# A linear-attention stage unrolled in turns of 16 slots

## The chip, the cores and the metric

The kernel runs on one core of one Trainium2 chip. The metric is the device time of one execution in microseconds (us), lower is better. A core has five engines with a queue each: TensorE (PE, matmuls; its weight loads are shown as PEld), VectorE (DVE), ScalarE (ACT), GpSimd (POOL) and SyncE (SP), which here only issues DMA transfers. Engines run side by side and wait for each other through semaphores. Each takes its own instructions strictly in the order of its list, so an instruction that waits holds up all behind it.

## What is computed

A decoder layer on x of shape (2, 2048, 512) in float32: linear attention, cross attention to a context of 154 keys, and a mixture of experts, each on a layer norm of its input and added to it. The change touches the first of the three:

```python
qkv = x @ w_qkv                                   # x is layer-normed
q, k, v = split(qkv), 16 heads of 32
q_proj = elu1(einsum('bhnd,hdf->bhnf', q, proj))  # elu1(x) = x + 1 if x > 0 else exp(x); 128 features
k_proj = elu1(einsum('bhnd,hdf->bhnf', k, proj))
kv     = einsum('bhnf,bhnd->bhfd', k_proj, v)
attn   = einsum('bhnf,bhfd->bhnd', q_proj, kv)
z      = 1 / (einsum('bhnf,bhf->bhn', q_proj, k_proj.sum(2)) + 1e-8)
out    = (attn * z) @ w_out + b_out
x      = x + out
```

## The kernel before

Four stages follow each other, each in a block of its own with its own semaphores: `project`, `attend_linear`, `attend_cross`, `experts`. `project` writes the queries of all tokens to DRAM and leaves kv and the key sums in SBUF. The 4096 tokens are 8 blocks of 512 (`NBLK`), four of each batch element.

`attend_linear` (L614) handles one block as follows.
- **Head** (L969): one matmul of the features' weights with the queries of a head (16 per block) into a PSUM bank. ACT takes relu(-x) (L771) and its exponential (L776) into a tile `e`; DVE adds max(x, 0) (L841) into `qp`.
- **Group** (L989, L983): for four heads, numerators and denominators, 8 matmul instructions each.
- **Divide** (L844): DVE adds 1e-8, takes the reciprocal (L848) and splits it into a high and a low part. Products in reduced precision are made from such parts: high x high, high x low, low x high (`PASSES`), so one product of four chunks is 12 matmuls.
- **Spread** (L1002): PE spreads the reciprocals over the rows, 8 matmuls; DVE multiplies the numerators by them (L860), ACT makes the high part (L787) and DVE the low part (L864) of `u_att`.
- **Output** (L1006): four tiles of 12 matmuls with `wo`; DVE adds each to x (L871) and takes its mean and variance (L873 to L878), POOL the power -1/2 (L761), DVE normalises (L884).
- **Transposes** (L1019): PE transposes each normalised tile, ACT and DVE make its high and low part (L791, L890).
- **Queries** of the cross attention (L1055): four groups of 12 matmuls with `wq`; DVE adds the bias (L921), SP stores all of them at once.

The order is written out by hand. A prologue does block 0 up to the spreading. Each `turn(i)` (L1023 on PE, L893 on DVE, L794 on ACT) then does output, transposes and queries of block i, and between them, in pairs, the heads of block i + 1, its groups, division and spreading. Turns run in loops of three (`Fori`) and one written out. All PSUM jobs but numerators and denominators go round four banks; PE waits until DVE has read the job four before. SP loads the queries of a block, 3 x 1 MB, when the heads of the block before are all computed (L739), and x of a block when its rows are normalised (L737). Semaphores are raised by one at the start of the stage in a block of their own (`prime`), since loops wait on register values.

Of the kernel before, what the change touches and what calls it, by code (L numbers as in the profile page):

```python
# [18 lines left out]
F32 = mybir.dt.float32  # L19
F32R = mybir.dt.float32r  # L20
# [129 lines left out]
def decoder_kernel(nc, a, out):  # L150
# [11 lines left out]
    with ExitStack() as whole:  # L162
# [4 lines left out]
        with ExitStack() as linear:  # L167

            kv_w = linear.enter_context(nc.sbuf_tensor("kv_w", [P, NB, H, HD], F32))
            ks_w = linear.enter_context(nc.sbuf_tensor("ks_w", [P, NB, H, HD], F32))  # L170
            project(nc, a, NBLK, BLK, x_blk, q_dram, ident, kv_w, ks_w, half, stage)
            attend_linear(nc, a, NBLK, BLK, x_blk, q_dram, x1_dram, xq_dram, ident, kv_w, ks_w, half, stage)
# [5 lines left out]
def project(nc, a, NBLK, BLK, x_blk, q_dram, ident, kv_w, ks_w, half, stage):  # L178
# [59 lines left out]
    with ExitStack() as ctx:  # L238
# [7 lines left out]
        f_w = sb("f_w", [3 * HD, H, F], F32R)  # L246
# [38 lines left out]
        with nc.Block() as block:  # L285
            @block.sync
            def _(sp):
# [32 lines left out]
                for i in range(-1, NBLK - 1):  # L320
# [4 lines left out]
                    if i == 0:  # L325
                        sp.wait_ge(w_lo, 3)
                        sp.dma_start(stage[0:3 * HD, 0:H * F], a["features3"]).then_inc(next_in, 16)
# [7 lines left out]
                sp.wait_ge(next_in, 48)  # L335
# [278 lines left out]
def attend_linear(nc, a, NBLK, BLK, x_blk, q_dram, x1_dram, xq_dram, ident, kv_w, ks_w, half, stage):  # L614

    qp_pair = lambda n: [("QP", 2 * n), ("QP", 2 * n + 1)]
    JOBS = (qp_pair(0) + [("O", 0)] + qp_pair(1) + [("O", 1)] + qp_pair(2)
            + [("O", 2)] + qp_pair(3) + [("T", 0), ("O", 3)] + qp_pair(4) + [("T", 1)] + qp_pair(5) + [("T", 2)]
            + qp_pair(6) + [("T", 3)] + qp_pair(7) + [("XQ", 0), ("XQ", 1), ("XQ", 2)]
            + [("R", g) for g in range(G)] + [("XQ", 3)])
    POS = {key: n for n, key in enumerate(JOBS)}
    LAST_POS = {key: n for n, key in enumerate(j for j in JOBS if j[0] not in ("QP", "R"))}
    NJ, BANKS, QSLOTS, ESLOTS = len(JOBS), 4, 8, 4  # L630
    FIRST = H + G
    assert NJ % BANKS == 0 and FIRST % BANKS == 0
    with ExitStack() as ctx:
# [3 lines left out]
        def sem(name):  # L637
            return primed(ctx, nc, sems, "li_" + name)

        sems = []  # L640
        f_w = sb("f_w", [3 * HD, H, F], F32R)
        wo = sb("wo", [P, 2, C, D], F32R)
        wq = sb("wq", [P, 2, C, D], F32R)
        spread_raw = sb("spread_raw", [P, G, P])
# [10 lines left out]
        e = sb("e", [P, ESLOTS, TB])  # L655
        num = sb("num", [P, G, TB])
        den = sb("den", [P, 2, TB])
        xq = sb("xq", [P, G, TB])
# [3 lines left out]
        pause = sb("pause", [P, 1])  # L662
        bank = [ctx.enter_context(nc.psum_tensor(f"li_bank{n}", [P, 512], F32)) for n in range(BANKS)]
        p_num = [ctx.enter_context(nc.psum_tensor(f"li_p_num{n}", [P, 512], F32)) for n in range(2)]
        p_den = ctx.enter_context(nc.psum_tensor("li_p_den", [P, 512], F32))

        w_hi, w_lo, const_in, next_in = sem("w_hi"), sem("w_lo"), sem("const_in"), sem("next_in")
        x_in, q_in, x1_out, xq_out = sem("x_in"), sem("q_in"), sem("x1_out"), sem("xq_out")
        q0_in = [sem(f"q0_in{g}") for g in range(G)]
        filled, dve_read = sem("filled"), sem("dve_read")  # L670
        relu_set, exp_set, heads_used = sem("relu_set"), sem("exp_set"), sem("heads_used")
        num_full, num_taken, den_set, rec_set = sem("num_full"), sem("num_taken"), sem("den_set"), sem("rec_set")
        norm_hi, norm_lo, turn_hi = sem("norm_hi"), sem("norm_lo"), sem("turn_hi")
        xb_set, stats_set, aggr_set, var_set = sem("xb_set"), sem("stats_set"), sem("aggr_set"), sem("var_set")
        rstd_set, xn_set = sem("rstd_set"), sem("xn_set")
        prime(nc, pause, sems)

        f_raw = stage[0:3 * HD, 0:H * F].rearrange("p (h f) -> p h f", h=H)

        def pos(turn):  # L680
            return LAST_POS if isinstance(turn, int) and turn == NBLK - 1 else POS

        def job(turn, key):

            return FIRST + NJ * turn + pos(turn)[key]

        def bank_of(turn, key):
            return bank[pos(turn)[key] % BANKS]

        def is_first(block):  # L690
            return isinstance(block, int) and block == 0

        def ahead(block, key):

            return key[1] + H * (key[0] == "R") if is_first(block) else job(block - 1, key)

        def bank_ahead(block, key):
            return bank[key[1] % BANKS] if is_first(block) else bank_of(block - 1, key)

        def turns(engine, body):  # L700

            for b in range(NBLK // BLK):
                with engine.Fori(0, BLK - 1) as k:
                    body(k + BLK * b, b, True)
                body(BLK * b + BLK - 1, b + 1, b + 1 < NBLK // BLK)

        with nc.Block() as block:
            @block.sync
            def _(sp):
                def load_q(i):  # L710
                    for r, part in enumerate((HI, LO, HI)):
                        sp.dma_start(q3[r * HD:(r + 1) * HD].bitcast(F32).rearrange("p h t -> p (h t)"),
                                     q_dram[i, part]).then_inc(q_in, 16)

                for g in range(G):
                    for r, part in enumerate((HI, LO, HI)):
                        cols = slice(g * HG * TB, (g + 1) * HG * TB)
# [26 lines left out]
                with sp.Fori(0, NBLK - 2) as i:  # L744
                    turn(i, 2)
# [1209 lines left out]
```

## Time and profile before

| | us |
|---|---|
| Median of 3 runs | 2795.8 (2794.68 to 2798.59) |
| Profiled execution | 2796.93 |
| Its span, first to last instruction | 2795.2 |
| PE busy over the span | 2638.4 (94%) |
| DVE, ACT, POOL busy | 1361.0, 858.0, 299.1 |
| Mean granted clock of PE | 0.959 |

The span is that of the profiled execution; the profile's times below are us from its start. The page shows PE busy nearly throughout, but the share is a mean over four stages. The slices of the linear stage, from about 460 to 845 us, have PE at 7 to 9 tenths, the ones of `experts` behind 1250 us at 9. A busy PE is also not always a fast one: the granted clock is 1.00 (2.4 GHz) or 0.50 (1.2 GHz), and a mean in between says that the stretch held both.

### The profile page before, as it was taken

What the parts mean: (1) busy time and instruction counts of PE and PEld (TensorE: products, weight loads), DVE (VectorE), ACT (ScalarE), POOL (GpSimd) and SP (SyncE); (2) the same over time, 40 slices, a digit from 0 to 9 for tenths busy, and PEclk for the clock granted to TensorE, in tenths of its full rate; (3) what the DMA queues carried; (4) which work ended last, traced back from release to release, by engine and by line L of the source; (5) the groups of instructions that cost most, each with busy time, mean ns of one, the idle gap of its engine ahead of it and who ended that gap; (6) DMA issues with size and microseconds to landing.
All of it is one profiled execution on the core that took longest, in us unless ns stands there. A gap on an engine that the chain in (4) does not pass through costs nothing. (4 is left out here: it accounts for less than half of the span.)

```text
span 2795.2 us, 34765 instructions
## 1 busy us (share of the span) xinstructions
PE 2638.4 (94%) x12656; PEld 1945.0 (70%) x12680; DVE 1361.0 (49%) x2100; ACT 858.0 (31%) x1364; POOL 299.1 (11%) x228
## 2 busy tenths in 40 slices
PE   7999997899896999799969999999998999999999
PEld 6777774556564554555458888888886888888887
DVE  4544434777765554655463344343335434334433
ACT  3555456455532332133221221111112121112111
POOL 1444343111110111111100000000000000000000
PEclk9999995999997999799989999999999999999999
DMA  6646434554613111212140000000113100000001
GB/s 193 170 98 148 107 87 113 158 156 115 166 75 110 61 54 45 92 61 91 46 155 23 23 23 32 36 23 23 45 45 136 42 26 23 23 23 23 23 23 60
DMA packets 61396, 207.62 MB, mean 74 GB/s; under 512 B 8592, under 2 KB 10384, under 8 KB 50192
## 3 DMA queue, kind: packets, MB, share of 16 engines
q1 hardware_dynamic: 61008, 205.59, 24.4%
q8 instruction: 63, 1.03, 0.2%
q0 software_dynamic: 288, 0.69, 0.1%
q14 instruction: 37, 0.30, 0.0%
HBM read 123.05 MB, written 58.72 MB: 65 GB/s over the span
## 5 line engine op out<-in xcount | busy, mean ns | idle before, releaser
L1876 PE MATMUL ex_pg<-ex_x,ex_w 128*128 128x512 f32 x3840 | 885.5, 390 | 3.3 <-DVE ex_lt L1759 3.3
L1876 PEld LDWEIGHTS ex_pg<-ex_x,ex_w 128*128 128x128 f32 x3840 | 723.3, 188 | 153.7 <-issue 3.5
L1891 PE MATMUL ex_pd<-ex_w,ex_ht 128*128 128x512 f32 x1920 | 446.6, 389 | 0.0
L1825 DVE TENSOR_TENSOR ex_h<-ex_s_g,ex_pg 128x512 f32<-128x512 f32 x160 | 110.1, 688 | 648.6 <-PE ex_pg L1876 647.7
L1891 PEld LDWEIGHTS ex_pd<-ex_w,ex_ht 128*128 128x128 f32 x1920 | 360.5, 188 | 74.7
L1732 ACT ACTIVATE ex_s_g<-ex_pg 128x512 f32<-128x512 f32 x160 | 95.8, 599 | 748.7 <-PE ex_pg L1876 748.6
L1797 DVE SCALAR_TENSOR_TENSOR ex_acc<-ex_pd,ex_share,ex_acc 128x512 f32<-128x512 f32 x320 | 234.4, 748 | 90.3 <-PE ex_pd L1891 84.9
L546 PE MATMUL pr_pj<-pr_xt,pr_w 128*128 128x512 f32 x768 | 194.5, 402 | 4.3 <-DVE pr_xt L443 4.2
L359 POOL TENSOR_TENSOR pr_ks_sum<-pr_ks_sum,pr_kp 128x512 f32<-128x512 f32 x128 | 164.5, 1286 | 228.2 <-DVE pr_kp L490 226.4
L490 DVE SCALAR_TENSOR_TENSOR pr_kp<-pr_pk,pr_kp 128x512 f32<-128x512 f32 x128 | 88.6, 692 | 179.5 <-ACT pr_kp L407 179.1
L546 PEld LDWEIGHTS pr_pj<-pr_xt,pr_w 128*128 128x128 f32 x768 | 142.1, 192 | 33.5 <-issue 2.2
L1263 ACT ACTIVATE cr_ring<-cr_s_bank 128x512 f32<-128x512 f32 x160 | 95.8, 599 | 202.7 <-remote 104.0
L1735 ACT CAST ex_ht<-ex_h 128x512 fp32r<-128x512 f32 x160 | 98.6, 616 | 181.4 <-DVE ex_h L1825 181.4
L1482 PE MATMUL cr_s_bank<-cr_xq,cr_k_w 128*128 128x512 f32 x480 | 151.7, 429 | 0.0
L1329 DVE TENSOR_REDUCE cr_mx<-cr_bank 128x4 f32<-128x512 f32 (+1 forms) x160 | 105.7, 688 | 93.9 <-PE cr_bank L1456 65.8
L404 ACT ACTIVATE pr_kp<-pr_pk 128x512 f32<-128x512 f32 x128 | 76.7, 599 | 133.9 <-PE pr_pk L576 126.8
L1828 DVE TENSOR_TENSOR ex_ht<-ex_h,ex_ht 128x512 fp32r<-128x512 f32 x160 | 110.4, 690 | 6.7
L1534 PE MATMUL cr_bank<-cr_wo,cr_u 128*128 128x512 f32 x384 | 99.9, 406 | 5.7 <-DVE cr_u L1398 5.7
L957 PE MATMUL li_bank<-li_u_ln,li_wq 128*128 128x512 f32 x384 | 97.4, 407 | 8.4 <-DVE li_u_ln L890 8.4
L1482 PEld LDWEIGHTS cr_s_bank<-cr_xq,cr_k_w 128*128 128x128 f32 x480 | 88.6, 193 | 22.0 <-issue 7.7
L841 DVE SCALAR_TENSOR_TENSOR li_qp<-li_bank,li_e 128x512 f32<-128x512 f32 x128 | 82.8, 685 | 33.7 <-ACT li_e L776 29.0
L543 PE MATMUL pr_pj<-pr_w,pr_xt 128*128 128x512 f32 x384 | 99.2, 400 | 0.0
(175 smaller groups left out, 2856.1 us busy)
## 6 DMA issues: line engine op xcount, KB each, us to landing
stage<-in_units SPq DMA_DIRECT2D x21, 1536.0 KB, 6.6
pr_k<-pr_kq SPq DMA_DIRECT2D x192, 128.0 KB, 2.5
li_q<-q_scratch SPq DMA_DIRECT2D x21, 1024.0 KB, 12.2
q_scratch<-pr_kq SPq DMA_DIRECT2D x128, 128.0 KB, 2.4
x_scratch<-cr_x SPq DMA_DIRECT2D x16, 1024.0 KB, 4.8
pr_x<-in_x SPq DMA_DIRECT2D x8, 1024.0 KB, 6.4
li_x<-in_x SPq DMA_DIRECT2D x8, 1024.0 KB, 5.2
x_scratch<-li_x SPq DMA_DIRECT2D x8, 1024.0 KB, 3.9
```

What stands on the lines that cost most here:

```text
L359: nc.gpsimd.tensor_tensor(part, part, slot(step), ALU.add).then_inc(ks_step, 1)
L543: mm = nc.tensor.matmul(out[:], xt[:, s, c, cols], w[:, m, 2, c], start=(n == 0), stop=(n == MM - 1))
L546: mm = nc.tensor.matmul(out[:], w[:, s, "QK".index(kind), c, cols], xt[:, m, c], start=(n == 0), stop=(n == MM - 1))
L1329: nc.vector.tensor_reduce(dst, src, AX.X, ALU.max).then_inc(dve_read, 1)
L1482: nc.tensor.matmul(s_bank[n % SBANKS][:], k_w[:, s, g, j * P:(j + 1) * P], q[:, m, g], start=(c == 0), stop=False)
L1534: mm = nc.tensor.matmul(bank_of(k, "O", t)[:], u[:, s, g, t * P:(t + 1) * P], wo[:, m, g], start=(n == 0), stop=(n == 3 * G - 1))
L1735: nc.scalar.copy(ht[:, s % 2, HI, f], h[:, f]).then_inc(ht_hi, 1)
L1797: nc.vector.scalar_tensor_tensor(acc[:, n], pd[t][:], share[:, n, bass.ds(e + s // BLK, 1)], acc[:, n], ALU.mult, ALU.add).then_inc(d_take ...
L1825: nc.vector.tensor_tensor(h[:, f], s_g[:, f], pg[2 * f + 1][:], ALU.mult).then_inc(h_set, 1)
L1828: nc.vector.tensor_tensor(ht[:, s % 2, LO, f], h[:, f], ht[:, s % 2, HI, f].bitcast(F32), ALU.subtract).then_inc(ht_lo, 1)
L1876: mm = nc.tensor.matmul(pg[2 * f + which][:], w[:, slot, sp_, col:col + P], x3[:, m, k, c * TB:(c + 1) * TB], start=(n == 0), stop=(n == 3 ...
L1891: mm = nc.tensor.matmul(pd[t][:], ht[:, s % 2, sp_, f, t * P:(t + 1) * P], w[:, slot, m, WD + f * D:WD + (f + 1) * D], start=(n == 0), sto ...
```

## The change

`attend_linear` is rewritten. There is no prologue and no loop: `turns` walks i from -1 to 8, and each turn has 16 slots. Slot s of turn i holds head s of block i + 1, and besides it parts of the output work of block i and of the queries of block i - 1. PE's part of each slot is in `PLAN`; the numbers are (kind, index, first matmul, last matmul):

```diff
+    PLAN = {
+        0: [("XQ", 0, 0, 8)],
+        1: [("ND", 3), ("XQ", 0, 8, 11)],
+        2: [("XQ", 0, 11, 12), ("XQ", 1, 0, 7)],
+        3: [("XQ", 1, 7, 12), ("XQ", 2, 0, 3)],
+        4: [("XQ", 2, 3, 12)],
+        5: [("R", 0), ("R", 1), ("R", 2)],
+        6: [("ND", 0), ("R", 3), ("XQ", 3, 0, 6)],
+        7: [("XQ", 3, 6, 12)],
+        8: [("O", 0, 0, 9)],
+        9: [("O", 0, 9, 12), ("O", 1, 0, 6)],
+        10: [("ND", 1), ("O", 1, 6, 9)],
+        11: [("O", 1, 9, 12), ("O", 2, 0, 6)],
+        12: [("O", 2, 6, 12), ("O", 3, 0, 3), ("T", 0)],
+        13: [("O", 3, 3, 12), ("T", 1)],
+        14: [("ND", 2), ("T", 2)],
+        15: [("T", 3)],
+    }
```

XQ are queries of block i - 1, ND is a group (of block i + 1, but group 3 of block i), R spreading, O output tiles and T transposes of block i. On PE a slot begins with its head:

```diff
+                def slot(i, s, ahead, now, behind):
+                    if ahead:
+                        head(i + 1, s)
+                    for job in PLAN[s]:
...
```

DVE's slot has the head first and then the rest of the slot:

```diff
+                def slot(i, s, ahead, now, behind):
+                    if s == 0 and behind:
+                        turned(i - 1, TT - 1)
+                    if ahead:
+                        n = H * (i + 1) + s
+                        dve.wait_ge(exp_set, n + 1)
+                        nc.vector.scalar_tensor_tensor(qp[:, n % QSLOTS], h_bank[n % HBANKS][:], 0.0, qp[:, n % QSLOTS],
+                                                       ALU.max, ALU.add).then_inc(qp_set, 1)
...
+                    if now:
+                        if s in (2, 3):
...
+                            reciprocal(i, s - 2)
+                        if s == 3:
+                            reciprocal_low(i, 0)
+                        if s == 4:
+                            reciprocal_low(i, 1)
+                        if s in (5, 6, 7):
+                            for g in ((0, 1), (2,), (3,))[s - 5]:
+                                normalise(i, g)
+                        if s in (10, 12, 13, 14):
+                            add_out(i, (10, 12, 13, 14).index(s))
+                        if s in (11, 13, 14, 15):
+                            norm(i, (11, 13, 14, 15).index(s))
+                        if s in (13, 14, 15):
+                            turned(i, s - 13)
```

ACT does relu and exponential of a head one right after the other, into `qp` itself (the tile `e` is gone), and takes over the high part of the reciprocal and the queries' bias:

```diff
+                        nc.scalar.activation(qp[:, n % QSLOTS], h_bank[n % HBANKS][:], ACT.Relu, scale=-1.0)\
+                            .then_inc(relu_set, 1)
+                        act.wait_ge(relu_set, n + 1)
+                        nc.scalar.activation(qp[:, n % QSLOTS], qp[:, n % QSLOTS], ACT.Exp, scale=-1.0)\
+                            .then_inc(exp_set, 1)
+                    if i == -1 and s == 6:
+                        nc.scalar.copy(wo[:, HI], staged(stage, 1)).then_inc(wo_hi, 1)
+                    if i == 0 and s == 0:
+                        nc.scalar.copy(wq[:, HI], staged(stage, 2)).then_inc(wq_hi, 1)
...
+                    if now and s == 2:
+                        take_num(i, G - 1)
+                    if behind and s in (3, 4):
+                        query(i - 1, s - 3)
+                    if now and s in (3, 4):
+                        reciprocal_high(i, s - 3)
+                    if behind and s == 5:
+                        query(i - 1, 2)
+                    if now and s in (5, 6, 7):
+                        for g in ((0,), (1, 2), (3,))[s - 5]:
+                            normalised(i, g)
+                    if behind and s == 8:
+                        query(i - 1, 3)
+                    if ahead and s in (8, 11, 15):
+                        take_num(i + 1, (8, 11, 15).index(s))
+                    if now and s in (13, 14, 15):
+                        turned(i, s - 13)
```

POOL takes the low part of `u_att` from DVE. The rest:
- Heads have two PSUM banks of their own (`HBANKS`), all other jobs share three (`BANKS`) instead of four for both.
- The reciprocal is taken in two halves of 256 columns, slots 2 and 3.
- SP loads the queries of block i + 2 in four parts, in slots 4, 8, 12 and 15 of turn i, each when the heads that used that part are computed; it stores the queries of the cross attention in four parts, in slots 3, 4, 5 and 8; x goes out in slot 14 and the next x comes in in slot 15.
- `f_w`, the features' weights split in two parts, is kept from `project` instead of being loaded and split again, and the priming block of this stage is gone.

```diff
+                    if behind and s in (3, 4, 5, 8):
+                        query_out(i - 1, (3, 4, 5, 8).index(s))
+                    if i >= 0 and i + 2 < NBLK and s in (4, 8, 12, 15):
+                        load_q(i + 2, (4, 8, 12, 15).index(s))
```

## Rows read from the trace of the kernel before

**Rows 1.** Busy times of one turn: length, PE, PEld, DVE, ACT, POOL, clock, DMA.

```profile
545.70:590.50 44.80, 41.08 (x200) 25.62 (x201) 34.19 (x61) 23.40 (x44) 7.53 (x5) 0.96 0.53 140
```

**Rows 2.** PE's waits from 480 to 845 us: total, times, longest.

```profile
PE li_bank L969 <- DMA li_q<-q_scratch: 8.9, 7, 1.7
PE li_bank L957 <- DVE li_u_ln L890: 8.4, 8, 1.4
```

**Rows 3.** Timeline of PE, one turn: start, length, instruction, idle before.

```profile
545.75 0.72 PE L969 MATMUL li_bank<-li_q,li_f_w 96*128 96x512 f32 x2 [1.52 <-DMA li_q<-q_scratch]
...
562.11 1.06 PE L989 MATMUL li_p_num<-li_qp,kv_w 128*32 128x512 f32 x8
562.99 1.04 PE L983 MATMUL li_p_den<-li_qp,ks_w 128*32 128x512 f32 x8
563.96 0.66 PE L1019 MATMUL li_bank<-ident,li_xn 128*128 128x128 f32 x4
564.37 1.10 PE L969 MATMUL li_bank<-li_q,li_f_w 96*128 96x512 f32 x2
...
584.30 2.00 PE L1002 MATMUL li_bank<-li_rec,li_spread 128*128 128x512 f32 x8
586.14 2.95 PE L957 MATMUL li_bank<-li_u_ln,li_wq 128*128 128x512 f32 x12
590.51 0.73 PE L969 MATMUL li_bank<-li_q,li_f_w 96*128 96x512 f32 x2 [1.42 <-DMA li_q<-q_scratch]
```

**Rows 4.** The same view, the last turn.

```profile
810.74 8.57 PE L957 MATMUL li_bank<-li_wo,li_u_att 128*128 128x512 f32 x36
819.14 0.60 PE L1019 MATMUL li_bank<-ident,li_xn 128*128 128x128 f32 x4
...
826.13 0.63 PE L1019 MATMUL li_bank<-ident,li_xn 128*128 128x128 f32 x4 [0.42 <-DVE li_xn L884]
828.16 14.21 PE L957 MATMUL li_bank<-li_u_ln,li_wq 128*128 128x512 f32 x48 [1.40 <-DVE li_u_ln L890]
```

**Rows 5.** Timeline of ACT and of DVE in the project stage.

```profile
301.99 0.60 ACT L404 ACTIVATE pr_kp<-pr_pk 128x512 f32<-128x512 f32 x1 [1.35 <-PE pr_pk L576]
302.63 0.63 ACT L407 ACTIVATE pr_kp<-pr_kp 128x512 f32<-128x512 f32 x1
...
303.29 0.69 DVE L490 SCALAR_TENSOR_TENSOR pr_kp<-pr_pk,pr_kp 128x512 f32<-128x512 f32 x1 [0.97 <-ACT pr_kp L407]
```

**Rows 6.** Timelines of PE and ACT: a head and its relu, twice.

```profile
549.11 0.63 PE L969 MATMUL li_bank<-li_q,li_f_w 96*128 96x512 f32 x2
...
549.54 1.09 ACT L771 ACTIVATE li_e<-li_bank 128x512 f32<-128x512 f32 x2 [1.14 <-PE li_bank L969]
...
463.59 2.04 PE L969 MATMUL li_bank<-li_q,li_f_w 96*128 96x512 f32 x4 [9.07 <-DMA li_q<-q_scratch]
...
464.39 1.09 ACT L771 ACTIVATE li_e<-li_bank 128x512 f32<-128x512 f32 x2 [4.68 <-PE li_bank L969]
```

**Rows 7.** Timeline of DVE: an output tile added, its normalisation, and one later.

```profile
557.90 0.69 DVE L871 TENSOR_TENSOR li_x<-li_x,li_bank 128x512 f32<-128x512 f32 x1 [1.80 <-PE li_bank L957]
...
559.71 0.54 DVE L884 TENSOR_SCALAR li_xn<-li_x,li_mv,li_rstd 128x512 f32<-128x512 f32 x1
...
825.45 0.54 DVE L884 TENSOR_SCALAR li_xn<-li_x,li_mv,li_rstd 128x512 f32<-128x512 f32 x1
```

**Rows 8.** Groups of instructions: count, busy, mean ns of one, idle before.

```profile
L359 POOL TENSOR_TENSOR pr_ks_sum<-pr_ks_sum,pr_kp 128x512 f32<-128x512 f32 x128 | 164.5, 1286 | 228.2 <-DVE pr_kp L490 226.4
...
L758 POOL TENSOR_TENSOR li_x<-li_x,li_bias 128x2048 f32<-128x2048 f32 x8 | 36.7, 4592 | 84.9 <-DMA li_x<-in_x 84.9
L848 DVE RECIPROCAL li_den<-li_den 128x512 f32<-128x512 f32 x8 | 26.8, 3353 | 0.3
```

**Rows 9.** As rows 1, two stretches of 3 us of the last turn.

```profile
825.70:828.70 3.00, 1.18 (x6) 0.92 (x6) 1.67 (x3) 1.17 (x2) 0.00 (x0) 0.79 0.29 120
828.70:831.70 3.00, 3.00 (x8) 2.31 (x7) 0.00 (x0) 0.00 (x0) 0.00 (x0) 0.50 0.00 0
```

## Prediction: what the slots make of the time

> **What bounds the kernel now.** I read the busy time by turn first, then the waits of TensorE (PE), then the timelines of PE, ScalarE (ACT) and VectorE (DVE) over one turn. Only the linear-attention stage changes, so only that stage is costed. Its first head product starts at 463.59 us [rows 6] and its last turn starts at 810.74 us [rows 4]. A full turn takes 590.51 - 545.75 = 44.8 us [rows 3], with PE busy 41.1 of it and DVE only 34.2 [rows 1]: PE is the bound, with gaps. The gaps that recur are the wait for the queries' load (8.9 us in seven turns) and the wait for the low part of the normalised rows (8.4 us in eight) [rows 2]. The six turns from 545.75 to 810.74 mean 44.2 us.
>
> PE's own work in a turn, by start to start: the output product and the queries are 96 matmuls at (819.14 - 810.74)/36 = 0.233 us [rows 4], so 22.5. Sixteen heads at the same pace are 3.8. A group of four heads costs 0.88 for numerators and 0.97 for denominators [rows 3], four groups 7.4. Four transposed tiles at 0.41 [rows 3] are 1.7. Spreading the reciprocals takes 1.84 [rows 3]. Sum 37.2 us; so about 7 us of each turn is gap or half clock, which is all that this change could win per turn.
>
> **The change part by part.** The PE work is the same 37.2 us, reordered. What decides is what each slot waits for.
>
> *Loads.* Queries now come in four parts, each requested as soon as its heads are consumed. The load wait (about 1.3 us a turn [rows 2]) goes to nothing, hidden behind three quarters of a turn. Query outputs go out in quarters, from ACT instead of DVE: four operations of 0.6 us more, and ACT was busy 23.4 of 44.8 us [rows 1]. SyncE's list mixes these stores, which wait for ACT, with the loads; the store of x stands last in the turn and behind it the next input, which is wanted some 20 us later, so nothing in that queue is late.
>
> *The new head step.* Per head, ACT does relu, then the exponential on the same tile at once, then DVE adds. The project stage does exactly this: relu to exponential 0.64 us, exponential to DVE 0.66 us [rows 5]. A head product starts 0.43 us before its relu at full clock and 0.80 at half clock [rows 6]. So DVE can take head s 1.73 us after PE started it and is free about 0.60 later: at +2.33. In DVE's list of a slot the head comes first, and everything else of the slot queues behind it.
>
> *Slots 13 and 14.* Adding an output tile, with its statistics, takes 559.71 - 557.90 = 1.81 us and the normalisation 0.54 more [rows 7]. In slot 13 DVE does head, output tile 2, normalisation of tile 1; PE in the same slot wants the transpose of tile 1. It may start at 2.33 + 1.81 + 0.54 + 0.14 = 4.8 us (0.14 for the semaphore, estimated from 825.99 to 826.13 in the last turn, where the normalisation ends and the transpose starts [rows 4, 7]). PE has only 0.23 + 9 x 0.233 = 2.3 us to do until then: stall 2.5. Slot 14 has the same pattern (output tile 3, normalisation 2, transpose 2) against a head and a group, 2.1 us: stall 2.7.
>
> *Slot 15 and the hand-over.* Head, normalisation 3, transpose 3: 2.33 + 0.54 + 0.14 = 3.0 us against a head alone, 0.23: stall 2.8. From the start of the last transpose to the queries that need its low part takes 828.16 - 826.13 = 2.0 us [rows 4], minus 0.6 of transpose and head: stall 1.4, what the kernel before pays too.
>
> *Slot 12.* Transpose 0 needs the bank of output tile 1, which DVE frees at slot start + 2.33 + 0.7 = 3.0; PE arrives at 2.3: stall 0.7.
>
> *Slots 2 to 5.* DVE's chain is head 2 (ready 1.73 after its start), denominator 0.7, half a reciprocal 1.7 (3.353 for a whole one [rows 8]), head 0.6, the other half 1.7, a low part 0.4, head 0.6, low part 0.4: the spreading product may start 8.5 us after slot 2 began. PE has slots 2 to 4 (6.6 us) and one head, so 6.8: stall 1.7. Slot 9 waits for the last low part of the attention result, now on GpSimd (POOL): four of 1.29 us, by the row of the same shape [rows 8]. The last starts after head 7, its multiplication on DVE and its cast on ACT, about 5.0 us after slot 7 began at 18.6: done by 23.6 us of the turn, against 22.8 at which PE asks. Stall 0.8.
>
> Sum of a turn at full clock: 37.2 + 0.7 + 2.5 + 2.7 + 2.8 + 1.4 + 1.7 + 0.8 = 49.8 us.
>
> *The clock.* In the last turn of before PE was busy 1.18 of 3 us, and the next 3 us were granted 0.50 (1.2 GHz of 2.4) [rows 9]; the 48 query matmuls at that place took 14.2 us against 11.2 at the pace above [rows 4]. Slots 13 to 15 now hold 6 us of work in 15.5, so I take the fall in every turn: 3.0 for the queries and 2 x 0.37 for later relus. A turn then takes 53.5; I take 53, since a fall that comes late costs less. The Trainium skill (TensorE: Matmul & The Clock Gate, section on oscillation) says that gaps between bursts of matmuls drop the clock and each new burst pays for the ramp. By that rule this order, meant to be denser or not, loses; the row of the last turn agrees.
>
> *Start.* The weights of the head product are no longer split again, but PE waited for the queries' load at that time [rows 6], so nothing; one block of semaphore priming goes, my estimate 1.5 us (bounds 0 and 3, as the gap between two stages is all that holds it). Only two head banks remain: head product to free bank is 0.80 + 0.64 + 0.66 + 0.73 = 2.83 us at half clock, so 1.42 a head, and each group (3.6 at half clock, by twice the rows of a group [rows 3]) stops the heads for about 2: 16 x 1.42 + about 4 = 27 us to turn 0. In turn 0 the split of the queries' weights on DVE (2.4 us, an estimate from 0.69 for a quarter of the columns [rows 5]) and the reciprocal chain come before the spreading: about 15 us, then 13 to slot 9, then 28 for slots 9 to 15 as above. The first query product starts 84 us after the first head. Before has its block 0 and turn 0 done, queries included, 545.75 - 463.59 = 82.2 us after it.
>
> *End.* Turn 7 has no heads: queries of block 6 (14.2), a group 1.85, spreading 1.84, 0.4 waiting, then outputs and transposes as in the last turn, 828.16 - 810.74 = 17.4: 35.7. The last queries take 14.2, as before. The last output is a quarter and lands about 1.5 us earlier.
>
> **The total.** -1.5 + 84 + 6 x 53 + 35.7 + 14.2 - 1.5 = 449 us. Before, the same stretch is 842.4 - 463.6 = 379 (the last queries start at 828.16 and take 14.21 [rows 4]). The difference is +70 us. The profiled execution took 2796.9 us (span 2795.2); the median is 1.1 below, so 2796.9 + 70 - 1.1 = 2866 us.
>
> **Rivals.**
> *The clock holds.* The same stalls without half clock: a turn of 49.8, turn 7 at 32.7, the start 2 us shorter: +70 - 19 - 3 - 2 = +46, so 2842 us. Against: rows 9. Chance 0.12.
> *The chain is tighter than I think* (faster than before). The mechanism: head products are answered ahead of PE, so that DVE reaches slots 13 to 15 early and PE finds its transposes ready. It decides from a turn of 41.3 us, where -1.5 + 84 + 6T + 35.7 + 14.2 - 1.5 equals 379; that leaves at most 4 us a turn for stalls and half clock. If the gaps of slots 13 to 15 and the clock loss vanish and the rest stays, a turn is 37.2 + 0.7 + 1.4 = 39.3, and turn 0 is some 8 us shorter: -20, so 2776 us. For it: PE was 92% busy in a turn already [rows 1], and loads are ahead. Against: PE issues head s in slot s and DVE cannot pass it; the slots' order is fixed on all engines. Chance 0.05, and 0.03 that it stops half-way, within 0.2%.
> *POOL collides.* The input's bias addition (4.6 us [rows 8]) and the low parts share POOL, and it also runs beside DVE. I reckon that it ends about 6 us before the first low part of the attention result is wanted. If the next input lands 10 us later, that margin is gone and slot 9 waits 4 us more in six turns: +24, 2890 us. The Trainium skill (SBUF — State Buffer, on the port pair shared by VectorE and GpSimd) says a DVE operation with two inputs in SBUF and a GpSimd operation that reads it exclude each other. By that rule the two short low parts of the reciprocal could wait for the addition, up to 4.6 us a turn, and the time would be 2866 + 6 x 4.6 = 2894 us as an estimate from that page. No row here has the two together. Chance 0.08.
> The forecast itself: 0.72.
>
> **How the numbers follow.** The range of 8 in 10 takes the forecast's own bounds (a turn from 51 to 56, so -12 and +18, start from 80 to 88) and the case of the held clock: 2836 to 2890. The chances: slower 0.92, same 0.03, faster 0.05. A difference under 0.2% is about what a measurement here cannot tell from none.
>
> **What would show it.** In the changed profile: turns (from one first query product to the next) of about 53 us; PE waiting for DVE's normalised tile (the transposes) for about 8 us a turn, by far its largest wait, three times a turn; the spreading product waiting 1.7 us for the reciprocal's low part; no wait for the queries' load; a granted clock of half at the end of each turn. A turn below 45 us, or transposes that do not wait, would prove the walk through the slots wrong.

## The result and the profile after

The changed kernel takes 2876.75 us (median of 6 runs, 2873.7 to 2881.31) against 2797.65 (2794.68 to 2799.49) on the same chip: ratio 1.0285, interval 1.0272 to 1.0298. It is slower by 79 us; the forecast was 70, and 2876.75 lies inside the range. Its profiled execution has a span of 2876.6 us (before 2795.2). By stages:

| us, profiled execution | before | after | difference |
|---|---|---|---|
| first head product | 463.59 | 463.61 | 0.0 |
| from there to the first product of cross attention | 396.1 | 482.9 | +86.8 |
| cross attention, to the first product of `experts` | 568.6 | 560.1 | -8.5 |
| `experts` | 1367.0 | 1370.0 | +3.0 |

PE's waits in the linear stage (total, times, longest), which answer to [rows 2]:

```profile
PE li_bank L998 <- DVE li_xn L889: 47.6, 23, 2.7
PE li_h_bank L952 <- DVE li_qp L904: 22.5, 11, 8.2
PE li_bank L976 <- DVE li_rec L862: 11.0, 7, 2.1
PE li_bank L1011 <- DVE li_u_ln L895: 9.3, 8, 1.5
PE li_bank L989 <- POOL li_u_att L771: 6.9, 8, 1.9
PE li_h_bank L952 <- DMA li_q<-q_scratch: 6.6, 1, 6.6
PE li_bank L998 <- DVE li_x L875: 4.5, 7, 0.7
```

In the changed kernel L998 is the transposes, L952 a head, L976 the spreading, L1011 the queries, L989 the output. No turn waits for the queries' load any more; the 6.6 us are the wait ahead of the stage's first head, 9.1 us in the kernel before [rows 6]. The transposes now wait 23 times for the normalised tile, 47.6 us in all. The busy times of one turn, as in [rows 1]:

```profile
555.69:610.11 54.42, 43.81 (x201) 27.46 (x201) 28.92 (x53) 28.52 (x51) 12.45 (x9) 0.88 0.57 176
```

The turn takes 54.4 us instead of 44.8. PE's busy time grew by 2.7 us though its work is the same, and the clock is 0.88 instead of 0.96. The end of that turn on PE, slots 12 to 15 (start, length, instruction, idle before it and who ended it), against [rows 3]:

```profile
592.69 0.66 PE L998 MATMUL li_bank<-ident,li_xn 128*128 128x128 f32 x4 [0.65 <-DVE li_x L875]
593.11 0.48 PE L952 MATMUL li_h_bank<-li_q,f_w 96*128 96x512 f32 x1
593.43 2.26 PE L989 MATMUL li_bank<-li_wo,li_u_att 128*128 128x512 f32 x9
598.09 0.97 PE L998 MATMUL li_bank<-ident,li_xn 128*128 128x128 f32 x4 [2.40 <-DVE li_xn L889]
598.72 0.77 PE L952 MATMUL li_h_bank<-li_q,f_w 96*128 96x512 f32 x1
599.42 1.94 PE L961 MATMUL li_p_den<-li_qp,ks_w 128*32 128x512 f32 x8
601.13 1.29 PE L967 MATMUL li_p_num<-li_qp,kv_w 128*32 128x512 f32 x8
603.98 0.63 PE L998 MATMUL li_bank<-ident,li_xn 128*128 128x128 f32 x4 [1.57 <-DVE li_xn L889]
604.37 0.48 PE L952 MATMUL li_h_bank<-li_q,f_w 96*128 96x512 f32 x1
607.53 1.09 PE L998 MATMUL li_bank<-ident,li_xn 128*128 128x128 f32 x4 [2.68 <-DVE li_xn L889]
608.26 0.78 PE L952 MATMUL li_h_bank<-li_q,f_w 96*128 96x512 f32 x1
610.11 3.75 PE L1011 MATMUL li_bank<-li_u_ln,li_wq 128*128 128x512 f32 x8 [1.06 <-DVE li_u_ln L895]
```

And DVE in slot 13, between the head at 593.11 and the transpose at 598.09:

```profile
594.98 0.69 DVE L904 SCALAR_TENSOR_TENSOR li_qp<-li_h_bank,li_qp 128x512 f32<-128x512 f32 x1 [1.15 <-ACT li_qp L822]
595.59 0.68 DVE L875 TENSOR_TENSOR li_x<-li_x,li_bank 128x512 f32<-128x512 f32 x1
...
597.39 0.55 DVE L889 TENSOR_SCALAR li_xn<-li_x,li_mv,li_rstd 128x512 f32<-128x512 f32 x1
```

This is the walk of the prediction: DVE waits for the head it was just given, then adds an output tile that nobody wants yet, then normalises the tile that PE stands waiting for. The clock at the end of the turn, answering to [rows 9] (length, busy PE, PEld, DVE, ACT, POOL, then the clock):

```profile
607.21:610.21 3.00, 1.62 (x6) 1.17 (x6) 1.46 (x3) 1.53 (x3) 0.00 (x0) 0.50 0.96 216
610.21:613.21 3.00, 3.00 (x7) 2.34 (x8) 0.69 (x1) 0.19 (x1) 0.00 (x0) 0.50 0.75 276
```

The queries begin at half clock in each of the seven turns: their eight matmuls take 3.4 or 3.75 us where later ones take 2.03.

### The profile page after: what moved, and what is told of

Same layout as the page of the kernel before. It is cut to its first block and busy times, and to the rows that moved or that the text cites. A ratio compares the mean times of both kernels' runs of the same rounds, so it can differ in the third digit from the quotient of the medians.

```text
span 2876.6 us, 34102 instructions
## 1 busy us (share of the span) xinstructions
PE 2666.4 (93%) x12680; PEld 1955.0 (68%) x12680; DVE 1315.4 (46%) x2043; ACT 897.6 (31%) x1411; POOL 337.9 (12%) x260
## 5 line engine op out<-in xcount | busy, mean ns | idle before, releaser
L904 DVE SCALAR_TENSOR_TENSOR li_qp<-li_h_bank,li_qp 128x512 f32<-128x512 f32 x128 | 87.8, 687 | 186.1 <-ACT li_qp L822 186.1
L489 DVE SCALAR_TENSOR_TENSOR pr_kp<-pr_pk,pr_kp 128x512 f32<-128x512 f32 x128 | 88.5, 692 | 181.3 <-ACT pr_kp L406 180.8
L819 ACT ACTIVATE li_qp<-li_h_bank 128x512 f32<-128x512 f32 x128 | 76.3, 596 | 171.6 <-PE li_h_bank L952 171.6
L1011 PE MATMUL li_bank<-li_u_ln,li_wq 128*128 128x512 f32 x384 | 112.2, 441 | 9.3 <-DVE li_u_ln L895 9.3
L1011 PEld LDWEIGHTS li_bank<-li_u_ln,li_wq 128*128 128x128 f32 x384 | 80.2, 213 | 37.7 <-DVE li_u_ln L895 12.8
```

The costliest lines, as they stand in the source:

```text
L1011: mm = nc.tensor.matmul(bank_of(i, "XQ", g)[:], wq[:, s, c, g * P:(g + 1) * P], u_ln[:, m, c], start=(n == 0), stop=(n == MM - 1))
```

## The experiments

Each kernel's time is compared with the kernel before on the same chip.

| kernel | median us | ratio to before, interval |
|---|---|---|
| after (again) | 2877.37 | 1.0289 (1.0269 to 1.0309) |
| spreading matrix alone | 2871.25 | 1.0265 (1.0243 to 1.0288) |
| low parts on DVE | 2865.93 | 1.0247 (1.0223 to 1.027) |
| fillers | 2855.56 | 1.0217 (1.0194 to 1.024) |
| output ahead of the head | 2830.77 | 1.0123 (1.0101 to 1.0145) |
| that with fillers | 2822.01 | 1.0091 (1.0072 to 1.011) |
| three edits together | 2812.2 | 1.0059 (1.0041 to 1.0078) |
| before, loads in parts | 2782.44 | 0.9949 (0.9936 to 0.9963) |
| replanned | 2772.65 | 0.992 (0.9901 to 0.994) |

### Output work ahead of the head

Does the order within DVE's slot make the stalls? In slots 12 to 15 the output tile and the normalisation go ahead of the head, an output tile one slot earlier; PE's order is untouched.

```diff
+                    if now and s >= 12:
+                        if s in (12, 13, 14):
+                            add_out(i, s - 11)
+                        if s >= 13:
+                            norm(i, s - 12)
                     if ahead:
```

> The changed kernel, with one change on VectorE: in slots 12 to 15 the output tile's addition and the normalisation stand ahead of the head instead of behind it. All work and all waits remain. My theory (the transposes wait because the head comes first in VectorE's slot): the waits of the transposes for the normalised tile, 47.6 us in all, fall to under 10 us, the turn goes from 54.4 to about 43.5 us, and the time to about 2803 us (2790 to 2820). Rival (the turn is long because only two banks serve the heads, and each head must be answered before the one after next): VectorE now answers heads later, so the turn stays at 54 us or grows, 2870 us or more.

Measured 2830.77 us, 46 less than after, but above the 2790 to 2820 expected. Turns are (834.31 - 548.60)/6 = 47.6 us, not 43.5. PE's waits:

```profile
PE li_bank L1016 <- DVE li_u_ln L895: 16.6, 8, 2.4
PE li_bank L1003 <- DVE li_xn L889: 13.0, 16, 2.1
```

The transposes' wait fell from 47.6 to 13.0 us: DVE's order was the cause of most of it. The two head banks are untouched, so it was not they that made it. Two things came short. The wait at the hand-over to the queries grew (1.06 to 2.13 us a turn), since ACT and DVE have the parts of two tiles to make in less time (in the 3 us ahead of the queries, 592.90 to 595.90, ACT is busy 2.97); and the clock is half again when the queries begin, although no gap in slots 13 to 15 is longer than 0.79 us and the hand-over is 2.13:

```profile
592.88 0.63 PE L1003 MATMUL li_bank<-ident,li_xn 128*128 128x128 f32 x4 [0.78 <-DVE li_xn L889]
595.87 3.75 PE L1016 MATMUL li_bank<-li_u_ln,li_wq 128*128 128x512 f32 x8 [2.13 <-DVE li_u_ln L895]
```

### More work in the gaps

What does the half clock cost? Products whose results are overwritten at once are put where PE would stand: six before each of transposes 1 to 3, three before the first query product. What is computed is the same.

```diff
+                def filler(out, n):
+                    for _ in range(n):
+                        nc.tensor.matmul(out, wo[:, HI, 0, 0:P], wo[:, HI, 0], start=True, stop=True)
...
+                    if t and i < NBLK - 1:
+                        filler(bank_of(i, "T", t)[:], 6)
```

> The changed kernel, with more work on TensorE: 6 products whose results are overwritten ahead of each of the transposes 1 to 3, and 3 ahead of the first query product, in turns 0 to 6. They fall into the stalls and wait for nothing new. Theory (each turn loses 4 to 5 us to half clock because TensorE idles in slots 13 to 15): the granted clock stays near 1.00, a turn falls from 54.4 to 50 us, the time to about 2848 us though there is more work. Rival (the half clock falls into the stalls and costs nothing, or the filler cannot hold the clock): a turn stays at 54.4 us or grows, 2877 to 2890 us.

Measured 2855.56 us: 21 less than after, with 21 more matmuls a turn. The clock and the first queries of a turn:

```profile
604.21:860.25 256.04, 225.21 (x1105) 145.01 (x1105) 144.61 (x265) 141.60 (x249) 62.38 (x45) 0.99 0.39 112
...
604.21 2.13 PE L1019 MATMUL li_bank<-li_u_ln,li_wq 128*128 128x512 f32 x8 [0.47 <-DVE li_u_ln L895]
```

Turns with the clock held take 50.9 us (604.21 to 655.11) against 54.4: the half clock costs 3.5 us a turn, and the stalls themselves the rest. One of the six turns still fell to half and took 52.4. Against the 2848 us expected, the turns with the clock held are 0.9 us longer than the 50 I had put (5.4 us in six), and this one adds 1.5.

### Both

Output work ahead of the head, with three fillers before each of transposes 1 to 3 and eight before the first query product.

```diff
+                        filler(bank_of(i, "T", t)[:], 3)
...
+                            filler(bank_of(i, "XQ", g)[:], 8)
```

> The kernel of e1 (output work ahead of the head in slots 12 to 15), with 3 products ahead of each of the transposes 1 to 3 and 8 ahead of the first query product, all overwritten. e1 had turns of 47.6 us where I expected 43.5. Theory (what is missing is half clock, which still came in every turn, behind a wait of 2.1 us at the hand-over to the queries): the clock holds, the first 8 query products take 2.1 instead of 3.8 us, a turn falls by 2 to 3 us to about 45, the time from 2831 to about 2814 us. Rival (the missing part is waits, which the filler lengthens): no gain, 2831 us or more.

Measured 2822.01 us, turns of 45.4 (595.53 to 822.38 are five), clock 1.00 over them. The half clock was worth 47.6 - 45.4 = 2.2 us a turn in the kernel with output first, as its shortfall said; 2.2 of 4.1, the rest being the longer hand-over and the transposes' remaining waits. The time came 8 above what was expected: one turn, the first, still took 47.7, and in the profiled execution cross attention took 567.0 us against 562.8 in the kernel without fillers, `experts` 1370.6 against 1366.4 (see the last section).

### The start: who waits for the constants

The prediction's start was 8 us short. PE after the first heads, and DVE there:

```profile
476.61 1.30 PE L952 MATMUL li_h_bank<-li_q,f_w 96*128 96x512 f32 x2 [8.19 <-DVE li_qp L904]
...
475.43 0.43 DVE L908 CAST li_spread<-li_den 128x512 fp32r<-128x512 f32 x1 [7.86 <-DMA li_bias<-in_b_out]
```

In slot 1 DVE copies the spreading matrix, and for that it waits until all three constants have landed (one semaphore, 48), the last of which SP issues behind the first queries' four loads. Heads 2 and later queue behind it. The edit gives that load a semaphore of its own:

```diff
-                sp.dma_start(spread_raw.rearrange("p g n -> p (g n)"), a["spread"]).then_inc(const_in, 16)
+                sp.dma_start(spread_raw.rearrange("p g n -> p (g n)"), a["spread"]).then_inc(spread_in, 16)
...
-                        dve.wait_ge(const_in, 48)
+                        dve.wait_ge(spread_in, 16)
```

> The changed kernel, with a semaphore of its own for the load of the spreading matrix. In the changed kernel VectorE's copy of that matrix, second in its list, waits for three constants, the last of which is queued behind the queries, 7.9 us. Theory (that wait stops the heads of block 0 and is all of the 8 us by which the start took longer than I forecast): 7 us less, about 2870 us. Rival (the loads of the later queries arrive too late anyway, so the heads would wait for them): 0 to 3 us less.

Measured 2871.25 us, 5.5 to 6 less than after. The 8.2 us wait is gone (the longest for `li_qp` is now 2.4), and the heads of block 0 take 31.7 us (463.95 to about 495.7) instead of 37.7: of the 7.9 us that DVE stood, 6.0 shortened the way to turn 0. PE's waits for `li_qp` went only from 22.5 to 18.7 us, in 14 pieces instead of 11. Part of that is a new wait. DVE now comes to the low part of `wo` while POOL adds the bias to x, and the same instruction that took 2.28 us in the changed kernel takes 5.55, with the next heads behind it:

```profile
478.93 4.53 POOL L768 TENSOR_TENSOR li_x<-li_x,li_bias 128x2048 f32<-128x2048 f32 x1 [29.40 <-DMA li_x<-in_x]
...
480.06 5.55 DVE L911 TENSOR_TENSOR li_wo<-stage,li_wo 128x2048 fp32r<-128x2048 f32 x1
```

It ends 2.15 us after POOL's (last section). The first query product comes 552.41 - 463.95 = 88.5 us after the first head. In the changed kernel that was 92.1 us in one profiled execution and 95.0 in the other, the difference being clock in turn 0, so a single trace tells this distance only within 3 us. The gain at the heads and the medians agree at 6.

### Low parts back on DVE

```diff
-                        nc.gpsimd.tensor_tensor(u_att[:, LO, g], num[:, g], u_att[:, HI, g].bitcast(F32), ALU.subtract)\
...
+                            for g in ((0,), (1, 2), (3,))[s - 5]:
+                                dve.wait_ge(norm_hi, G * i + g + 1)
+                                nc.vector.tensor_tensor(u_att[:, LO, g], num[:, g], u_att[:, HI, g].bitcast(F32),
```

> The changed kernel, with the low parts of the attention result back on VectorE, as before. Theory (GpSimd's slower operation costs only the 0.8 us wait of slot 9, and its work beside VectorE disturbs nothing): 0.6 us a turn, 4 us in all, about 2873 us. Rival (GpSimd's work holds up VectorE or the input's addition): more than 10 us less.

Measured 2865.93 us, 11 less, not 4. The wait of the first output tile at slot 9 is gone in all full turns:

```profile
PE li_bank L989 <- DVE li_u_att L927: 1.6, 2, 1.5
```

From the first head to the first product of cross attention the two profiled executions differ by 12.1 us. Six turns of 53.0 instead of 54.4 are 8.3 of it, the wait in front of cross attention 3.4 (last section), and the start only 0.4 (91.7 us from the first head to the first query product, for 92.1). Of the 1.4 us a turn 0.8 is the wait. The other 0.6 goes with an earlier return of the clock in every second turn, where the eight queries took 3.5 to 3.6 us instead of 3.75. Why the clock returns earlier was not tested; the changed kernel has one such turn in six, and its second profiled execution has turns of 54.1. The gain is of the size that the rival named, but its mechanism is not seen: DVE's additions for the heads take 0.69 us beside POOL's low parts as they do alone, and POOL's addition of the input takes 4.6 us in both kernels.

### The three edits together

Output work ahead of the head, the semaphore of the spreading matrix, and the low parts on DVE.

> The edits of e1, e2 and e4 together, no other. If their causes are independent, their gains add (46 + 5.5 + 10.8): about 2814 us. If they share one cause, such as the clock at the end of the turn, it is 2820 us or more.

Measured 2812.2 us. The single gains, 46.6, 6.1 and 11.4 from 2877.37, would give 2813.3: they add, so each is a cause of its own and none hid another. 14 us remain to the kernel before, and the transposes still wait 13.1 us and the hand-over 16.6.

### Replanned

The spreading semaphore and the low parts on DVE as above, and each step moved so that what it needs was finished a slot before. On DVE the output tiles come a slot earlier and ahead of the head. On PE the spreading comes one or two slots later, the first transpose in front of the last output tile, and two groups behind transposes, so that PE has work in front of its waits. There are also 12 tiles instead of 8 for the heads' features (`QSLOTS`).

```diff
-    SLOTS, QSLOTS, HBANKS, BANKS = H, 8, 2, 3
+    SLOTS, QSLOTS, HBANKS, BANKS = H, 12, 2, 3
...
+        6: [("XQ", 3, 9, 12), ("R", 0), ("R", 1), ("ND", 0)],
...
+        12: [("T", 0), ("O", 3, 0, 9)],
+        13: [("O", 3, 9, 12), ("T", 1), ("ND", 1)],
+        14: [("T", 2)],
+        15: [("T", 3), ("ND", 2)],
```

> A version meant to beat both: the changed kernel with the start of e2, the low parts of e4, 12 tiles for the heads' features instead of 8, and the slots replanned: output tiles a slot earlier on VectorE and ahead of the head, two of the four groups moved behind the last output tile (one ahead of the last transposes, one between the last transpose and the queries), and the fourth query group ahead of the spreading. If the order of the slots is the whole cause, the waits of slots 12 to 15 shrink to about 1 us and the clock holds: a turn of 39 to 41 us against 44.2 before and 54.4 after, and 2775 to 2785 us. If the form itself (two head banks, relu and exponential one behind the other) costs time, it stays above 2796 us.

Measured 2772.65 us (2771.08 to 2775.7), 25 less than before. Its turns and the end of one:

```profile
578.30:781.99 203.69, 194.28 (x1000) 127.83 (x1000) 154.22 (x285) 142.88 (x250) 36.77 (x25) 1.00 0.49 141
...
615.25 0.63 PE L1013 MATMUL li_bank<-ident,li_xn 128*128 128x128 f32 x4 [0.20 <-DVE li_xn L885]
...
619.05 1.17 PE L1026 MATMUL li_bank<-li_u_ln,li_wq 128*128 128x512 f32 x4 [0.90 <-DVE li_u_ln L891]
```

Five turns take 40.74 us each at full clock. The 16 slots, the two head banks and the three for the rest were not at fault: a kernel that has all of them takes 40.7 us a turn instead of 54.4. Which of the moves gave how much of the 40 us between the three edits and this kernel was not separated, nor were the 12 tiles tried alone. Not all of the 25 us are the turns' own: up to the first product of cross attention the stage takes 380.6 us against 396.1, so 15.5, and cross attention 560.4 against 568.6.

### The kernel before, with its loads in parts

What is the good part of the change worth by itself? The kernel before loads its queries in four parts, each when its heads are computed; nothing else differs.

```diff
+                    def parts(lo, hi):
+                        for g in range(lo, hi):
+                            if left > 1:
+                                sp.wait_ge(filled, 2 + job(i, ("QP", HG * g + HG - 1)))
+                                load_q(i + 2, g)
...
-                    if lo == 0 and not is_first(i):
-                        pe.wait_ge(q_in, 1 + 48 * i)
```

> The kernel before with one part of the change alone: the queries of the next block but one are loaded in four parts, each when its heads are computed. Theory (the loads are the one thing that the change improves, and its worth is the wait of 8.9 us in seven turns): that wait vanishes from the trace, and the time falls by 6 to 9 us, about 2789 us. Rival (the wait is covered by another, such as the low part of the attention result, or the loads collide with the stores): the wait moves elsewhere, 0 to 3 us less.

Measured 2782.44 us: 14.2 less than before, above the 6 to 9 expected. PE waits for the load twice, both at the start of the stage (10.8 us, 9.4 the longest), no longer at each turn; four turns of six take 41.6 us and two 43.2. The waits were 8.9 us; the rest of the gain, about a third, is the clock. The same group of a turn, before and with loads in parts:

```profile
568.20 1.93 PE L989 MATMUL li_p_num<-li_qp,kv_w 128*32 128x512 f32 x8 [0.18 <-DVE li_qp L841]
```

```profile
565.55 1.06 PE L996 MATMUL li_p_num<-li_qp,kv_w 128*32 128x512 f32 x8 [0.17 <-DVE li_qp L848]
```

Over the turns the clock is 0.99 instead of 0.97. It falls in two of six turns (those of 43.2 us) instead of five. Why is not shown: only one of the five falls comes right behind the wait for the load (at 680.6 us). The other four come, like the two that are left, 22 us behind it, after transposes and single heads, the last head behind a wait of 0.85 us before and 0.87 here. So the new order costs not 79 but 2876.75 - 2782.44 = 94 us against what the loads alone would have brought.

This kernel also puts the replanned one in its place. From the first head to the first product of cross attention it takes 378.4 us, the replanned one 380.6: its turns are longer (42.1 us against 40.7), but its first query product comes 62.6 us after the first head against 73.8. The 10 us by which the replanned kernel is faster lie outside that stretch: in the profiled executions it is 3.0 us ahead there already, and gains 6.5 in cross attention and 3.7 in `experts`, whose code is the same. So no run shows that the new form, even replanned, gains anything in its own stage over the old one with its loads in parts.

### The changed kernel once more

> The changed kernel itself, to compare the others with it on one chip: 2877 us, turns of 54.4 us.

Measured 2877.37 us on the second chip, ratio 1.0289: the comparisons of the two groups can be put side by side. The profiled executions of the one kernel also show how far a single trace carries. The first query product comes 92.1 us after the first head in one and 95.0 in the other, turns take 54.4 and 54.1, and `experts` 1370.0 and 1366.4.

## Why the prediction was right, point by point

**The turn: right.** Forecast 53, measured (882.09 - 555.69)/6 = 54.4 us. Each stall came in the place and at nearly the size that the walk gave. Slot 12: 0.7, measured 0.65. Slot 13: 2.5, measured 2.40. Slot 15: 2.8, measured 2.68. Hand-over: 1.4, measured 1.06. Spreading: 1.7, measured 1.48 to 1.53. Slot 9: 0.8, measured 0.77. Slot 14: 2.7, measured 1.57, because the group ahead of it ran at half clock (599.42 to about 602.4) and filled the rest. The 1.4 us missed are three terms: the clock cost 3.5 us (kernel with fillers) where I took 3.2; the work is 37.8 us where I took 37.2, since the spreading, cut in two by a head, takes 1.47 + 0.57 = 2.04 us from start to start instead of 1.84, and a head in front of a transpose or a group 0.32 instead of 0.23; and what is left, 54.4 - 3.5 - 37.8 = 13.1, is stalls, where the seven terms gave 12.6 (the profile counts a wait from the end of the last matmul, some 0.16 us after the next could have started).

**The clock: right in its mechanism, and now measured.** [Rows 9] gave one fall behind sparse transposes; in the new order the clock falls in every turn. These turns agree with the rule of the Trainium skill (TensorE: Matmul & The Clock Gate, section on oscillation) that each burst behind a gap starts slow again, though no gap here is longer than 2.7 us and the page's example has longer ones. The fillers turned it round, and more work took less time. The rival "the clock holds" at 2842 us fell: the clock did not hold, and where fillers hold it in five of six turns the kernel takes 2856 us.

**The start: wrong by 8 us (84, measured 92.1).** The four terms of the start add up to 83, not 84. I costed the head steps of turn -1 and left out what DVE does between them. The step "16 x 1.42 + about 4 = 27 us to turn 0" took 37.7 us (463.61 to about 501.3). The copy of the spreading matrix behind its semaphore is 6.0 of the 10.7 missed, by the experiment. The rest is the groups in the heads' way:

```profile
483.74 1.22 PE L952 MATMUL li_h_bank<-li_q,f_w 96*128 96x512 f32 x2
486.61 0.80 PE L952 MATMUL li_h_bank<-li_q,f_w 96*128 96x512 f32 x1 [1.65 <-DVE li_qp L904]
487.76 0.80 PE L952 MATMUL li_h_bank<-li_q,f_w 96*128 96x512 f32 x1 [0.35 <-DVE li_qp L904]
488.49 1.94 PE L961 MATMUL li_p_den<-li_qp,ks_w 128*32 128x512 f32 x8
490.19 1.93 PE L967 MATMUL li_p_num<-li_qp,kv_w 128*32 128x512 f32 x8
492.06 0.88 PE L952 MATMUL li_h_bank<-li_q,f_w 96*128 96x512 f32 x2
```

Four heads with their group take 8.3 us (483.74 to 492.06), the next four 8.7, where I had 27/4 = 6.8. The 2.83 us from a head product to its free bank is right (483.74 to 486.61), but a group adds 2.6 us (8.3 - 4 x 1.42) or 3.0. Three groups stand ahead of turn 0, some 8 us where I had "about 4", though my own 2 us a group would have made it 6. Against it, "13 to slot 9" took 8.7 (516.87 to 525.60). That term was too high in itself: a full turn, which has queries there, takes 9.6 us for the same slots (571.28 to 580.86). "15 to the spreading" took 15.5, "28 for slots 9 to 15" 30.1.

**The ends: right.** Turn 7 took 34.65 us for 35.7, the last queries 14.05 for 14.2. Behind them the wait to the first product of cross attention is 15.7 us instead of 17.3, the 1.5 us of the smaller last output.

**The priming: right in size, not seen in this execution.** From DVE's last copy of the project stage to the first head it was 9.0 us and is now 6.5, so 2.5 are gone; but `project` ended 2.5 us later in this execution (457.08 for 454.55), and the first head came at the same time. The scatter of the stage ahead is of the size of the term: in all nine profiled executions of the new form the first head comes at 460.9 to 464.0 (mean 462.3), in the two of the old form at 463.6 and 465.4.

**The loads: right in place, too small in size.** "About 1.3 us a turn" was counted as the wait alone, 8 to 9 us of the kernel. The loads in parts alone gave 14.2. The rest went with the clock, which fell in two of the six turns instead of five; what ties it to the load is open.

**The sum.** From the first head to the end of the last queries the forecast's terms are 84 + 318 + 35.7 + 14.2 = 451.9 us; measured 467.2 (463.61 to 930.79), 15.3 more: start 8.1, turns 8.4, ends -1.2. With the 1.5 us of priming not seen, and what I had not forecast at all, cross attention at -8.5 and `experts` at +3.0, it is 70 + 15.3 + 1.5 - 8.5 + 3.0 = 81.3, and the spans differ by 81.4. The +3.0 of `experts` is scatter, as the second profiled execution of the same kernel has 1366.4 us there. So the miss was larger than 79 against 70 looks: without the later stages' 5.5 us, which nobody forecast, the kernel would have stood near 2882 us, still in the range.

**The rivals.** "Tighter chain": refuted, transposes wait in every turn. Its price had a slip: it says that the stalls outside slots 13 to 15 stay, but its 39.3 us leave out the 1.7 of the spreading and the 0.8 of slot 9; with them it is 41.8, and the kernel some 15 us slower than the 2776 it gave. "POOL collides": the addition ends at 613.24 + 4.56 = 617.8 and the first low part starts at 628.14, so the margin of 6 us that I reckoned is 10, and the forecast 0.8 us at slot 9 stands. The rule of the Trainium skill (SBUF — State Buffer, on the shared port pair) did not come into play in this kernel: the low parts of the reciprocal start at 624.35, 6.5 us behind the addition's end, and never met it. In four of the variants a DVE operation with two inputs in SBUF did meet POOL's addition, and each time the trace agrees with the rule (last section).

## What to carry to other kernels

In a schedule cut into slots, an engine that answers another one should find each step's input finished one slot earlier; put what another engine is waiting for first in its list, and a step that waits for the newest product last. Price a stall twice where the clock is at stake: with what is idle and with what runs slowly behind it. Before rewriting an order for the sake of its loads, try the loads alone: here they gave 14 us by themselves, and no reordering got the stage below what they reached (378.4 us).

## What was not expected of the hardware

**DVE waited for POOL.** The low part of `wo` is one DVE instruction with both inputs in SBUF. In eight of the eleven traces it takes 2.28 to 2.29 us, and no POOL operation of a microsecond or more runs beside it. In the three with the spreading semaphore it starts while POOL's addition of the bias is running, and takes 5.55, 5.32 and 4.87 us, ending 2.15 to 2.16 us after POOL's end each time: it did next to nothing until POOL was done. In the replanned kernel PE stood 5.05 us behind it. The low parts of the reciprocal met the same addition twice (1.14 us with fillers, 0.81 in the replanned kernel, instead of 0.36 to 0.43) and ended 0.3 us after it. DVE's operations with one of two inputs in PSUM took no longer beside POOL: 0.69 us for a head's addition, 24 times in the changed kernel. So moving an earlier wait away can bring two engines together that had not met.

**Order of two loads.** Cross attention opens with a load of 640 KB issued by POOL and one of 576 KB by SP, for which PE waits. Where SP's is issued first it lands after 4.0 to 4.1 us (three kernels, those with the low parts on DVE), and PE waits 12.2 to 12.3 us; where POOL's is issued 0.3 us ahead of it, after 7.6 to 8.0 us (the eight others), and PE waits 15.5 to 17.7. No run changed this order alone. The kernel after, then the one with low parts on DVE:

```profile
938.17 0.73 POOL L1174 DMA_DIRECT2D cr_minus<-in_minus  x1
938.50 0.43 SPq L1127 DMA_DIRECT2D cr_ctx_t<-in_ctxT  x1
```

```profile
928.23 0.43 SPq L1127 DMA_DIRECT2D cr_ctx_t<-in_ctxT  x1
928.49 0.73 POOL L1174 DMA_DIRECT2D cr_minus<-in_minus  x1 [0.60 <-issue]
```

**Cross attention, whose code did not change,** took 560 to 563 us in eight profiled kernels of the new form and 567.0 in a ninth, against 568.6 and 566.9 in the two of the old form. Most of what differs is idle time of PE that nothing in the profile explains ("issue"): 8.7 us in two pieces before, 2.8 in one after, 6.0 in two in the ninth. The rest is PE's busy time, 520.5 us before and 517.7 after. The cause of both is open. The two pieces before:

```profile
1137.12 1.43 PE L1428 MATMUL cr_bank<-cr_ctx_t,stage 128*128 128x160 f32 x4 [4.39 <-issue]
1142.91 6.68 PE L1428 MATMUL cr_bank<-cr_ctx_t,stage 128*128 128x160 f32 x28 [4.36 <-issue]
```

**The clock fell behind gaps of at most 2.1 us** (2.4 in one turn) in the kernel with output first, with transposes and single heads between them, and held in the replanned one, whose gap at that place is 0.9 us (1.3 in one turn). The length of the gap alone does not decide: in the kernel before, the clock fell behind a gap of 0.85 us in four of six turns, and with loads in parts it held in four of six turns behind one of 0.87.
